# Routed layers: the shared pieces leave the expert loop, and the first 1024 tokens, not 512, are normalised behind it

## The chip, the cores and the metric

The kernel runs on one core of one Trainium2 chip. A core has five engines, each with its own in-order instruction stream: TensorE (PE), VectorE (DVE), ScalarE (ACT), GpSimd (POOL) and SyncE (SP, which here only issues DMAs). They meet through semaphores: an instruction that waits stops everything behind it on its own engine. The metric is the device time of the whole program in microseconds (us); lower is better.

## The reference, cut to what matters

2048 tokens of width 256 go through six layers in a row. Each layer normalises `x` and adds its result to `x`:

```
x = x + 0.5 * ffn0(layernorm(x))     # routed0: 16 experts, top 4 of 16 for each token, plus a shared gated MLP
x = x + attn0(layernorm(x))          # attention0: one head over 2048 tokens, causal
x = x + 0.5 * ffn0(layernorm(x))     # routed1: the same weights as routed0
x = x + 0.5 * ffn1(layernorm(x))     # gated0: silu(x Wg * gs) * (x Wu * us), then Wd
x = x + attn1(layernorm(x))          # attention1: 16 heads
x = x + 0.5 * ffn1(layernorm(x))     # gated1
```

In `ffn0` every expert takes at most 128 tokens: their rows are gathered, go through `silu(xg @ w_gate) * (xg @ w_up) @ w_down`, are weighted, and are scatter-added into `y`. The shared part is `silu(x @ sw_gate) * (x @ sw_up) @ sw_down` over all tokens.

## The kernel before

The six stages run one after another on each engine, with no barrier between them: an engine enters the next stage when its own stream does. `x` stays in on-chip memory as 16 tiles of 128 tokens. A **chunk** is 512 tokens (4 tiles), so there are four chunks, 0 to 3. Products in full precision are made of three matmuls over a high and a low part (`products`, L170 to L172).

**Normalising a chunk** (`ChunkNorm`) takes steps on every engine: DVE measures it (`dve_stats`, L245 and L249), POOL raises the variance to the power -0.5 (`pool_inverse`, L262 and L264; in `quick` chunks DVE then refines it, L285 to L291), DVE and ACT write two normalised tiles each (L309, L319), PE turns them (`pe_flip`, L326), ACT writes the high part of the turned chunk (L331) and DVE the low part (L337). A stage's first matmuls on a chunk need that low part.

**A routed stage** runs a fixed list of steps (`Routed.plan_order`), which every engine walks in the same order, doing its own share. The shared MLP is cut into pieces. Piece q (0 to 11, three for each chunk) has a `gate` step and an `up` step on PE, 12 matmuls in all; ACT takes the silu of the gate, DVE multiplies (L928, signal `acted`), then `round` splits the result: ACT L848, DVE L932. `sums` (c, half) are 18 matmuls on PE that finish half a chunk, and DVE adds them to `x` (L937, signal `added`). In the text g, u and s with numbers stand for these steps: g10, u10, s30 (chunk 3, first half).

The experts run in a loop: POOL gathers 128 rows of `xn_rows` (`fetch`, L1095, six buffers), PE turns them (`x`, L731), multiplies (`feed`, L740), turns back (`h`, L749), multiplies down (`down`, L760), and POOL scatter-adds the result with a DMA (`place`, L1102) into one of two arrays `y_rows` in memory, by turns. Place n waits until place n-2 has landed, and fetch n+6 stands just ahead of place n in POOL's stream.

Two constants cut the list of what is left of the shared pieces once the experts can begin: `AMONG` pieces are spread among the experts, `BEHIND` follow them, and two more are laid into the start of the loop. `early` is the number of `up` steps ahead of the experts; only those pieces alternate between two pairs of accumulator banks (`side`). Every later piece uses the first pair, and then u(q) waits until DVE has multiplied piece q-1, and g(q) until ACT has read gate q-1.

**The expert sums reach x** in six transfers and two DVE additions. Chunk 0 of both `y_rows` arrays is fetched into spare rooms by SP (L649) and added by DVE (`grow`, L987). Chunks 1 to 3 are accumulated straight into `x` by POOL's DMAs (`pool_grow`, L1127): first the half from `y_rows[0]`, and the half from `y_rows[1]` only after the first has landed. `GROWN` gives their order. Chunk 0 is normalised for the next stage (`self.first`) among the last pieces: POOL's part stands between the two transfers of chunk 1. Chunks 1 to 3 are normalised inside attention0 (`Attention0.plan_order`) and inside gated0 (the tables `GROWN_NORM` and `GROWN_LATE`, keys are chunk and piece).

In `gated0` each chunk has six pieces of up to 24 matmuls, `up` (c, m), with ACT's silu (L1890) and DVE's product (L1950) behind each; `up` (c, m) waits for the product two pieces back. ACT also rounds the down weights in chunk 0 (L1862), which waits for their load.

Of the kernel before, what the change touches and what calls it, by code (L numbers as in the profile page):

```python
# [100 lines left out]
class Core:  # L101
# [33 lines left out]
    def loads(self, name):  # L135

        return self.flag(name, 16)

    def keep_warm(self, pe, bank, count):

        for _ in range(count):
            pe.matmul(bank.rearrange("p (a b) -> p a b", b=P), self.ident_b[:], self.ident_b[:].unsqueeze(1).broadcast_to([P, BANK // P, P]),
                      start=True, stop=True)

# [243 lines left out]
class Routed:  # L388
# [6 lines left out]

    AMONG, BEHIND = 4, 12

    def __init__(self, core, stack, tag, then, kept, prior=None, start=None, ahead=()):
# [130 lines left out]
    def plan_order(self):  # L529
# [35 lines left out]
        for n in range(NE):  # L565
# [11 lines left out]
            if n < NE - 2:  # L577
# [78 lines left out]
    def pe(self, pe):  # L656
# [23 lines left out]
        for what, *key in self.order:  # L680
# [70 lines left out]
            elif what == "down":  # L751
                n = key[0]
                pe.wait_ge(*self.h_copied[tag, n])
                pe.wait_ge(*self.down_in[n % self.SLOTS][tag, n])
                if n >= 2:
                    pe.wait_ge(*self.weighed[tag, n - 2])
                elif n == 0 and self.early_sums:
                    pe.wait_ge(*self.added[(tag, *self.early_sums[-1])])
                for k in range(IK):
                    done = pe.matmul(self.down_ps[n % 2], self.e_cols[:, n % 2, k * P:(k + 1) * P], self.e_dn[:, n % self.SLOTS, k, :],  # L760
                                     start=k == 0, stop=k == IK - 1)
                done.then_inc(*self.e_downed.one)
            elif what == "flip":
                self.first.pe_flip(pe, 0, key[0], self.first_banks[key[0]])

# [41 lines left out]
    def act(self, act):  # L807
# [28 lines left out]
        for what, *key in self.order:  # L836
# [30 lines left out]
            elif what == "ahead":  # L867
                self.follower.act_ahead(act, *key)
            elif what == "scale":
                self.first.act_rows(act, 0)  # L870
            elif what == "flip":
                self.first.act_flip(act, 0, key[0], self.first_banks[key[0]])

# [20 lines left out]
    def dve(self, dve):  # L894
# [26 lines left out]
        for what, *key in self.order:  # L921
# [66 lines left out]
            elif what == "measure":  # L988
                self.first.dve_stats(dve, 0)
            elif what == "scale":  # L990
                self.first.dve_rows(dve, 0)
            elif what == "flip":
                self.first.dve_rest(dve, 0, key[0], self.first_banks[key[0]])
        self.step.totals[0] += self.steps
# [71 lines left out]
    def pool(self, pool):  # L1066
# [236 lines left out]
class Attention0(Softmax):  # L1303
# [18 lines left out]
    def __init__(self, core, stack, tag, then, kept, prior, add_y=False):  # L1322
# [41 lines left out]
    def plan_order(self):  # L1364
        project = lambda c: [("flip", c, 0), ("flip", c, 1), ("state", c), ("action", c)]

        order = [("stats", 1), ("inverse", 1), ("grow", 2), *project(0)[2:], ("values", 0), ("score", 0, 0, 0), ("peak", 0, 0), ("exp", 0, 0),
                 ("values", 1), ("bias", 0), ("grow", 3)]
        for t in range(NT + 1):

            nc = t // 4 + 1
            if nc < NCH and t % 4 == 0:
                order += [("rows", nc), ("bias", nc)]

# [4 lines left out]
            if nc < NCH and t % 4 == (nc > 1):  # L1379
                order += project(nc)[:2]  # L1380
            if nc < NCH and t % 4 == 1 + (nc > 1):
# [42 lines left out]
    def rests(self, c):  # L1424

        return (self.first if c == 0 else self.norm).lo[self.tag, c, HK - 1]

# [35 lines left out]
    def pool(self, pool):  # L1463
        for step in self.order:
# [6 lines left out]
            elif step[0] == "bias":  # L1471
                c = step[1]
                pool.wait_ge(*self.weights_in["bo"][self.tag])
                x = self.core.x[:, 4 * c:4 * c + 4, :]
                (self.norm if c else self.first).wait_rows(pool, c)
# [117 lines left out]
class Gated:  # L1593
# [23 lines left out]
    def __init__(self, core, stack, tag, prior, add_y=False, result=None, then=None, ahead=()):  # L1617
# [44 lines left out]
        self.norm = ChunkNorm(core, sb, tag, [c for c in range(NCH) if c not in ahead], add_y=add_y, by_act={**late, 1: 2} if add_y else late,  # L1662
                              quick=(1,) if add_y else ())
        self.first = prior.first if add_y else None
# [43 lines left out]

    def sp_ahead(self, sp):
        for m in range(4):  # L1710
            self.sp_up(sp, m)
# [47 lines left out]
    def pe(self, pe):  # L1759
        if self.add_y:  # L1760
            self.core.keep_warm(pe, self.up_ps[:, 3, :], 4)
        for c in range(NCH):
# [13 lines left out]
    def pe_up(self, pe, c, m):  # L1776
        core, tag, where = self.core, self.tag, slice(c * CH, (c + 1) * CH)
        if m == 0 and c == 0 and self.first:
            self.first.wait_turned(pe, c)
        elif m == 0:  # L1780
            self.norm.wait_turned(pe, c)
        if c == 0:
# [29 lines left out]
    def raw(self, m):  # L1812
        if m < 4 and self.add_y:
            return self.prior.norm.xn[:, 4:12, :].rearrange("p a h -> p (a h)").rearrange("p (k w) -> p k w", k=HK)[:, :, self.cols(m)]
        if m < 2:
# [92 lines left out]
    def dve(self, dve):  # L1908
        tag, norm = self.tag, self.norm
        if self.add_y:  # L1910
            norm.dve_stats(dve, 1)
        else:
            follow(dve, self.prior, "pool")
# [53 lines left out]
    def pool(self, pool):  # L1967
        tag = self.tag
        if self.add_y:
            self.prior.pool_grow(pool, 2)  # L1970
            self.prior.pool_grow(pool, 3)
            self.norm.pool_inverse(pool, 1)
        for m in range(4 if self.add_y else 2, I1M):
# [504 lines left out]
def program(nc, src, out):  # L2478
    with ExitStack() as stack:
# [98 lines left out]
```

## Time and profile before

| | us |
|---|---|
| median of 3 runs | 2030.62 |
| lowest, highest | 2028.19, 2030.73 |
| the profiled execution | 2029.83 |
| its span (first to last instruction) | 2028.0 |
| PE busy | 1944.3 (96% of the span) |
| DVE busy | 1431.3 (71%) |
| ACT busy | 1315.5 (65%) |
| POOL busy | 938.6 (46%) |
| mean granted clock of TensorE | 0.992 of full |

The profile gives each engine's busy time, the granted clock of TensorE in tenths of full speed (1.00 is 2.4 GHz, and 1.2 GHz reads as 0.50), and for each instruction what ended the idle time ahead of it. Seen over the span PE is nearly full. The stretches in which it isn't lie at the start and where the two routed stages hand over: routed0 to attention0 at about 120 to 170 us, routed1 to gated0 at about 360 to 430 us. Those are the two places that the change touches.

### The profile page before, as it was taken

Reading aid. Unit: us, or ns where it says so; the run is one execution under the profiler, and the core shown is the slowest. Engines: PE = TensorE matmul, PEld = TensorE weight load, DVE = VectorE, ACT = ScalarE, POOL = GpSimd, SP = SyncE. Lnnn points to the kernel's source line nnn. Section 1 sums busy time; section 2 is a strip of 40 time slices with the busy share of each in tenths; the row PEclk is TensorE's granted clock in tenths of the full one; section 3 lists DMA queues with packets and bytes.
Section 4 is the critical chain, followed back from the end, with each engine's and each line's share of the span. In section 5 each row is a group of like instructions: output and inputs, shape, how many; then the busy total and the mean of one; then the engine's idle time right before and its main releaser. Section 6 shows DMA issues by size and latency. Waiting matters only on the chain.

```text
span 2028.0 us, 40320 instructions
## 1 busy us (share of the span) xinstructions
PE 1944.3 (96%) x13766; PEld 1767.9 (87%) x13766; DVE 1431.3 (71%) x3604; ACT 1315.5 (65%) x3367; POOL 938.6 (46%) x956
## 2 busy tenths in 40 slices
PE   6988989898999999999999999999999999999999
PEld 4768867687899999999999999999999999998888
DVE  8358763655868777786877778687777878777753
ACT  4335623444778777777868777786777778676752
POOL 1642116434445536454553645455364454536242
PEclk9989999999999999999999999999999999999999
DMA  7751058600000000000000000000000000000000
GB/s 266 204 93 22 33 188 213 145 1 9 9 6 9 9 6 4 7 9 6 9 9 7 4 6 9 9 7 9 7 4 7 9 9 7 9 7 1 22 27 32
DMA packets 58601, 73.46 MB, mean 36 GB/s; under 512 B 9760, under 2 KB 45216, under 8 KB 58272
## 3 DMA queue, kind: packets, MB, share of 16 engines
q1 hardware_dynamic: 45920, 55.93, 8.5%
q0 software_dynamic: 12480, 14.95, 4.3%
q8 instruction: 114, 1.87, 0.4%
q14 instruction: 87, 0.71, 0.1%
HBM read 51.06 MB, written 19.80 MB: 35 GB/s over the span
## 4 chain that ended last, share of the span: by engine, by line
PE 60%; DVE 11%; ACT 9%; issue 7%; POOL 7%; DMA 5%; ACTq 0%; SPq 0%; POOLq 0%; DVEq 0%
PE phase_scores L1222 16%; PE phase_ring L1280 9%; PE phase_y L171 5%; PE phase_y L172 5%; PE phase_y L170 5%; PE phase_ring L170 4%; PE phase_ring L172 4%; PE phase_ring L171 4%; ACT phase_p L1254 3%; DMA y_rows<-phase_out,phase_rows 3%; DVE phase_scores L1233 2%; PE phase_up_ps L170 1%; POOL phase_rot L2456 1%; PE phase_up_ps L172 1%; PE phase_up_ps L171 1%
## 5 line engine op out<-in xcount | busy, mean ns | idle before, releaser
L1254 ACT ACTIVATE phase_p<-phase_scores,phase_bias 128x512 f32<-128x512 f32 (+3 forms) x680 | 416.9, 627 | 117.1 <-DVE phase_bias L1242 116.6
L1300 DVE TENSOR_TENSOR phase_pt_lo<-phase_ring,phase_pt_hi 128x512 fp32r<-128x512 f32 (+3 forms) x680 | 390.2, 602 | 89.5 <-ACT phase_pt_hi L1295 85.7
L1295 ACT ACTIVATE phase_pt_hi<-phase_ring 128x512 fp32r<-128x512 f32 (+3 forms) x680 | 342.9, 535 | 105.3 <-PE phase_ring L1280 101.7
L1280 PE MATMUL phase_ring<-sb_ident,phase_p 128*128 128x128 f32 x2312 | 340.3, 274 | 11.8 <-ACT phase_p L1254 6.8
L170 PE MATMUL phase_y<-phase_pt_hi,phase_v_hi 128*128 128x256 f32 (+1 forms) x1152 | 341.3, 296 | 6.5 <-DVE phase_y_lo L2430 6.5
L171 PE MATMUL phase_y<-phase_pt_lo,phase_v_hi 128*128 128x256 f32 (+1 forms) x1152 | 321.3, 279 | 0.0
L172 PE MATMUL phase_y<-phase_pt_hi,phase_v_lo 128*128 128x256 f32 (+1 forms) x1152 | 321.1, 279 | 0.0
L1280 PEld LDWEIGHTS phase_ring<-sb_ident,phase_p 128*128 128x128 f32 x2312 | 271.8, 140 | 51.8 <-ACT phase_p L1254 16.3
L1235 DVE TENSOR_REDUCE phase_peaks<-phase_scores 128x1 f32<-128x512 f32 (+1 forms) x408 | 265.6, 665 | 46.3 <-PE phase_scores L1222 43.9
L2454 POOL TENSOR_TENSOR phase_straight<-phase_rot,late_rope 64x512 f32<-64x512 f32 x128 | 163.5, 1277 | 274.5 <-ACT phase_rot L2323 274.4
L2471 POOL TENSOR_TENSOR sb_x<-sb_x,phase_part 128x512 f32<-128x512 f32 x128 | 165.0, 1289 | 252.9 <-ACT phase_part L2358 246.5
L1222 PE MATMUL phase_scores<-phase_k_hi,phase_q_hi 128*128 128x512 f32 (+3 forms) x640 | 250.7, 392 | 8.3 <-POOL phase_k_lo L2464 5.2
L1222 PE MATMUL phase_scores<-phase_k_hi,phase_q_lo 128*128 128x512 f32 (+3 forms) x640 | 232.3, 363 | 0.0
L1222 PE MATMUL phase_scores<-phase_k_lo,phase_q_hi 128*128 128x512 f32 (+3 forms) x640 | 231.5, 362 | 0.0
L170 PEld LDWEIGHTS phase_y<-phase_pt_hi,phase_v_hi 128*128 128x128 f32 x1152 | 217.9, 189 | 11.7 <-issue 9.7
L171 PEld LDWEIGHTS phase_y<-phase_pt_lo,phase_v_hi 128*128 128x128 f32 x1152 | 218.0, 189 | 1.4
L172 PEld LDWEIGHTS phase_y<-phase_pt_hi,phase_v_lo 128*128 128x128 f32 x1152 | 217.0, 188 | 0.0
L2456 POOL TENSOR_TENSOR phase_rot<-phase_straight,phase_crossed 64x512 f32<-64x512 f32 x128 | 164.2, 1283 | 10.0
L2463 POOL TENSOR_TENSOR phase_q_lo<-phase_rot,phase_q_hi 128x256 fp32r<-128x256 f32 x128 | 94.2, 736 | 147.7 <-ACT phase_k_hi L2333 144.4
L170 PE MATMUL phase_ring<-sb_xt_hi,late_qk_hi 128*128 128x256 f32 x512 | 147.3, 288 | 0.9 <-DVE phase_pt_lo L1300 0.7
L172 PE MATMUL phase_ring<-sb_xt_hi,late_qk_lo 128*128 128x256 f32 x512 | 143.3, 280 | 0.0
L171 PE MATMUL phase_ring<-sb_xt_lo,late_qk_hi 128*128 128x256 f32 x512 | 143.3, 280 | 0.0
(276 smaller groups left out, 4858.2 us busy)
## 6 DMA issues: line engine op xcount, KB each, us to landing
phase_e_up<-expert_up SPq DMA_DIRECT2D x32, 352.0 KB, 4.6
phase_e_dn<-expert_down SPq DMA_DIRECT2D x32, 256.0 KB, 5.1
y_rows<-phase_zero SPq DMA_DIRECT2D x16, 512.0 KB, 7.8
sb_x<-y_rows POOLq DMA_DIRECT2D x12, 512.0 KB, 6.3
xn_rows<-phase_ln_xn SPq DMA_DIRECT2D x8, 512.0 KB, 3.0
late_raw_qk<-qk SPq DMA_DIRECT2D x16, 256.0 KB, 2.7
sb_x<-x SPq DMA_DIRECT2D x4, 512.0 KB, 5.7
phase_e_up<-y_rows SPq DMA_DIRECT2D x4, 512.0 KB, 4.0
```

The lines of the kernel that those rows point to most:

```text
L170: pe.matmul(out, left_hi[c], r_hi, start=first and c == 0, stop=False)
L171: pe.matmul(out, left_hi[c], r_lo, start=False, stop=False)
L172: done = pe.matmul(out, left_lo[c], r_hi, start=False, stop=last and c == n - 1)
L1222: done = pe.matmul(self.scores[:, at:at + n], a, b, start=k == 0, stop=k == len(pairs(n)) - 1)
L1235: dve.tensor_reduce(peak, scores, AX.X, ALU.max).then_inc(*self.peaked.one)
L1254: act.activation(self.p[:, at:at + width], self.scores[:, at:at + width], ACT.Exp, bias=self.bias[:, t % 2:t % 2 + 1], accum_out=self.sums ...
L1280: done = pe.transpose(bank[:, j * P:(j + 1) * P], self.p[:, (4 * place + j) * P:(4 * place + j + 1) * P], self.core.ident[:])
L1295: act.activation(hi, value, ACT.Copy).then_inc(*self.t_hi.one)
L1300: dve.tensor_tensor(lo, value, as_f32(hi), ALU.subtract).then_inc(*self.t_lo.one)
L2454: pool.tensor_tensor(self.straight[:], self.rot[0:64], self.wide(slice(0, 64), g), ALU.mult).then_inc(*self.straightened.one)
L2456: pool.tensor_tensor(self.rot[0:64], self.straight[:], self.crossed[:], ALU.add).then_inc(*self.turned_by_rope.one)
L2471: pool.tensor_tensor(rows, rows, self.part[:], ALU.add).then_inc(*self.added.one)
```

## The change

`AMONG` goes from 4 to 0 and `BEHIND` from 12 to 20. Of the shared steps left when the experts begin, fewer come ahead (`early` falls from 6 to 4), none among them, and more behind. Chunk 1 is now normalised and turned in the routed stage too, by the same object as chunk 0, and the next stage starts with both. On POOL both transfers of chunk 1 now come ahead of the inverse of chunk 0. The four dummy matmuls at the start of attention0 and gated0 (`keep_warm`) are gone. In gated0 chunks 2 and 3 are measured, scaled and turned at earlier pieces, and its first four weight pieces are loaded into tiles 8 to 15 of the old normalised rows, so that SP waits for the last store and turn of those rows first.

```diff
-    AMONG, BEHIND = 4, 12
+    AMONG, BEHIND = 0, 20
...
-        self.first = ChunkNorm(core, sb, then, (0,), after=lambda c: self.grown[tag, 1], like=self.norm, quick=(0,))
-        self.first_banks = [banks[:, b, :] for b in (6, 7)]
+        self.first = ChunkNorm(core, sb, then, (0, 1), after=lambda c: core.loads("y_in1")[then] if c else self.grown[tag, 1], like=self.norm, quick=(0, 1))
+        self.first_banks = [[banks[:, b, :] for b in pair] for pair in ((6, 7), (5, 3))]
...
-        among = {("up", last - 3): [("ahead", 0)], ("round", last - 3): [("ahead", 1)], ("up", last - 2): [("ahead", 2)],
-                 ("round", last - 2): [("ahead", 3)], ("up", last): [("grow", 0)], ("round", last): [("grow", 1), ("measure",)],
-                 ("sums", NCH - 2, 1): [("scale",)], ("sums", NCH - 1, 1): [("flip", 0), ("flip", 1)]}
+        among = {("up", last - 5): [("ahead", 0)], ("round", last - 5): [("ahead", 1)], ("up", last - 4): [("ahead", 2)],
+                 ("round", last - 4): [("ahead", 3)], ("up", last - 3): [("grow", 0)], ("round", last - 3): [("grow", 1), ("measure", 0)],
+                 ("up", last - 2): [("scale", 0), ("measure", 1)], ("up", last - 1): [("scale", 1)],
+                 ("round", last - 1): [("flip", 0, 0), ("flip", 0, 1)], ("round", last): [("flip", 1, 0), ("flip", 1, 1)]}
...
         pool.wait_ge(*self.y_fetched[1][tag])
         self.pool_grow(pool, 0)
-        self.first.pool_inverse(pool, 0)
         pool.wait_ge(*self.placed[1][tag, NE - 1])
         self.pool_grow(pool, 1)
+        self.first.pool_inverse(pool, 0)
+        self.first.pool_inverse(pool, 1)
...
-        self.norm = ChunkNorm(core, sb, tag, range(1, NCH), add_y=add_y, quick=(1,),
+        self.norm = ChunkNorm(core, sb, tag, range(2, NCH), add_y=add_y,
...
-        core.keep_warm(pe, self.scores[:, 3 * BANK:], 4)
...
-    GROWN_NORM = {(0, 1): [("scale", 0, 1)], (0, 2): [("turn", 0, 1)], (1, 0): [("scale", 0, 2)], (1, 1): [("turn", 0, 2)],
-                  (1, 3): [("scale", 0, 3)], (1, 4): [("turn", 0, 3)]}
-    GROWN_LATE = {(0, 4): [("measure", 0, 2), ("invert", 0, 2)], (1, 1): [("measure", 0, 3), ("invert", 0, 3)]}
+    GROWN_NORM = {(0, 5): [("scale", 0, 2)], (1, 0): [("turn", 0, 2)], (1, 2): [("scale", 0, 3)], (1, 3): [("turn", 0, 3)]}
+    GROWN_LATE = {(0, 3): [("measure", 0, 2), ("invert", 0, 2)], (0, 5): [("measure", 0, 3), ("invert", 0, 3)]}
...
+        if self.add_y:
+            sp.wait_ge(*prior.norm.rows_out[prior.tag, NCH - 1])
+            sp.wait_ge(*prior.norm.turned[prior.tag, NCH - 1, HK - 1])
...
-            self.core.keep_warm(pe, self.up_ps[:, 3, :], 4)
...
-            norm.dve_stats(dve, 1)
...
-            gated0 = Gated(core, inner, "gated0", routed1, add_y=True, then="attention1", ahead=(0,))
+            gated0 = Gated(core, inner, "gated0", routed1, add_y=True, then="attention1", ahead=(0, 1))
```

The order of POOL's stream at the end of routed0, before (the first row is the last of the expert places; `DMA sb_x<-y_rows` is a transfer of `pool_grow`):

```order
L1102 DMA y_rows<-phase_out,phase_rows 2176x256 x7
L1127 DMA sb_x<-y_rows 128x4x256
L262 TENSOR_SCALAR phase_ln_var<-phase_ln_mv 128x4
L264 TENSOR_TENSOR phase_ln_rstd<-phase_ln_var,sb_half 128x4
L1127 DMA sb_x<-y_rows 128x4x256
```

The same place in the changed kernel:

```order
L1097 DMA y_rows<-phase_out,phase_rows 2176x256 x7
L1123 DMA sb_x<-y_rows 128x4x256 x2
L256 TENSOR_SCALAR phase_ln_var<-phase_ln_mv 128x4
L258 TENSOR_TENSOR phase_ln_rstd<-phase_ln_var,sb_half 128x4
L256 TENSOR_SCALAR phase_ln_var<-phase_ln_mv 128x4
L258 TENSOR_TENSOR phase_ln_rstd<-phase_ln_var,sb_half 128x4
```

The inverse of chunk 0 moved behind the second transfer, which itself waits for the landing of the first.

ACT's stream at the end of routed0, before (`phase_gate` is a gate's silu, `phase_h_hi` a round, `phase_ln_xn` the scaling of a chunk, `sb_xt_hi` its turned high part):

```order
L842 ACTIVATE phase_gate<-phase_banks 128x512
L848 ACTIVATE phase_h_hi<-phase_mul 128x512
L842 ACTIVATE phase_gate<-phase_banks 128x512
L848 ACTIVATE phase_h_hi<-phase_mul 128x512 x2
L319 ACTIVATE phase_ln_xn<-sb_x,phase_ln_shift,phase_ln_rstd 128x256 x2
L331 ACTIVATE sb_xt_hi<-phase_banks 128x512 x2
```

ACT's stream at the same end in the changed kernel:

```order
L837 ACTIVATE phase_gate<-phase_banks 128x512
L843 ACTIVATE phase_h_hi<-phase_mul 128x512
L313 ACTIVATE phase_ln_xn<-sb_x,phase_ln_shift,phase_ln_rstd 128x256 x2
L837 ACTIVATE phase_gate<-phase_banks 128x512
L843 ACTIVATE phase_h_hi<-phase_mul 128x512
L313 ACTIVATE phase_ln_xn<-sb_x,phase_ln_shift,phase_ln_rstd 128x256 x2
L837 ACTIVATE phase_gate<-phase_banks 128x512
L843 ACTIVATE phase_h_hi<-phase_mul 128x512
L325 ACTIVATE sb_xt_hi<-phase_banks 128x512 x2
L843 ACTIVATE phase_h_hi<-phase_mul 128x512
L325 ACTIVATE sb_xt_hi<-phase_banks 128x512 x2
```

Two gates, g10 and g11, now stand behind a scaling on ACT; before, the only scaling stood behind the last gate.

DVE's stream at the same end in the changed kernel (`phase_mul` is the product of u9, then of u10, `BN_STATS` the measuring of chunk 1):

```order
L923 TENSOR_TENSOR phase_mul<-phase_gate,phase_banks 128x512
L279 TENSOR_TENSOR phase_ln_tmp<-phase_ln_rstd 128x4
L281 SCALAR_TENSOR_TENSOR phase_ln_tmp<-phase_ln_tmp,phase_ln_var 128x4
L283 SCALAR_TENSOR_TENSOR phase_ln_rstd<-phase_ln_tmp,phase_ln_rstd 128x4
L285 SCALAR_TENSOR_TENSOR phase_ln_shift<-phase_ln_mv,phase_ln_rstd 128x4
L303 TENSOR_SCALAR phase_ln_xn<-sb_x,phase_ln_mv,phase_ln_rstd 128x256 x2
L239 BN_STATS phase_ln_stats<-sb_x 128x6 x4
L243 BN_AGGR phase_ln_mv<-phase_ln_stats 128x2 x4
L927 TENSOR_TENSOR phase_h_lo<-phase_mul,phase_h_hi 128x512
L923 TENSOR_TENSOR phase_mul<-phase_gate,phase_banks 128x512
```

The measuring of chunk 1, which before was the first work of the next stage, now stands between the products of u9 and u10.

## Rows read from the trace of the kernel before

**Rows 1.** Timeline of PE around expert 0 of routed0 (start us, us, instruction).
```profile
53.06 0.39 PE L170 MATMUL phase_banks<-sb_xt_hi,kept_up_hi 128*128 128x512 f32 x1
54.45 0.28 PE L170 MATMUL phase_banks<-kept_dn_hi,phase_h_hi 128*128 128x256 f32 x1
...
59.29 0.38 PE L731 MATMUL phase_banks<-sb_ident,phase_x_rows 128*128 128x128 f32 x2
```

**Rows 2.** Timeline of POOL, the first fetch of routed0, and its line's landing time.
```profile
53.23 1.26 POOL L1095 DMA_INDIRECT phase_x_rows<-xn_rows,phase_rows  x1 [32.52 <-DVE phase_rows L1064]
...
DMA to landing us min/median/max: 3.1/3.1/3.1
```

**Rows 3.** The same for routed1, with PE's first turn of an expert.
```profile
295.11 1.14 POOL L1095 DMA_INDIRECT phase_x_rows<-xn_rows,phase_rows  x1 [30.89 <-DVE phase_rows L1064]
...
DMA to landing us min/median/max: 3.8/3.8/3.8
...
301.28 0.38 PE L731 MATMUL phase_banks<-sb_ident,phase_x_rows 128*128 128x128 f32 x2
```

**Rows 4.** Line L1102 (places), landing time: ten from 68 us, then five from 102 us.
```profile
DMA to landing us min/median/max: 4.5/5.7/6.8
...
DMA to landing us min/median/max: 3.7/3.8/3.9
```

**Rows 5.** The chain that ended last, around the last place (start us, us, what).
```profile
115.41 5.92 DMA y_rows<-phase_out,phase_rows
121.35 3.80 DMA phase_e_up<-y_rows
```

**Rows 6.** Timeline of POOL, chunk 1's two transfers, and their line's landing time.
```profile
125.44 1.39 POOL L1127 DMA_DIRECT2D sb_x<-y_rows  x1 [8.20 <-DMA phase_e_up<-y_rows]
...
128.66 1.05 POOL L264 TENSOR_TENSOR phase_ln_rstd<-phase_ln_var,sb_half 128x4 f32<-128x4 f32 x1
131.84 1.38 POOL L1127 DMA_DIRECT2D sb_x<-y_rows  x1 [2.13 <-DMA sb_x<-y_rows]
...
DMA to landing us min/median/max: 5.8/6.0/6.2
```

**Rows 7.** Timeline of DVE and of ACT at the end of routed0.
```profile
118.57 0.69 DVE L928 TENSOR_TENSOR phase_mul<-phase_gate,phase_banks 128x512 f32<-128x512 f32 x1
...
126.43 1.40 DVE L245 BATCH_NORM_STATS2 phase_ln_stats<-sb_x 128x6 f32<-128x256 f32 x4
...
136.41 1.08 ACT L331 ACTIVATE sb_xt_hi<-phase_banks 128x512 fp32r<-128x512 f32 x2 [4.79 <-PE phase_banks L326]
```

**Rows 8.** Timeline of PE, the start of attention0.
```profile
138.38 0.50 PE L170 MATMUL phase_ring<-sb_xt_hi,phase_hi_ws 128*128 128x512 f32 x1 [0.71 <-DVE sb_xt_lo L337]
...
148.65 1.94 PE L326 MATMUL phase_ring<-sb_ident,phase_ln_xn 128*128 128x128 f32 x8 [3.28 <-ACT phase_ln_xn L319]
...
156.26 0.33 PE L1222 MATMUL phase_scores<-phase_a,phase_s 128*128 128x384 f32 x1
```

**Rows 9.** Busy time by window: PE, PEld, DVE, ACT, POOL, granted clock, DMA share, GB/s.
```profile
129.00:135.00 6.00, 6.00 (x30) 6.00 (x31) 2.41 (x8) 1.09 (x2) 2.09 (x2) 0.54 0.53 78
...
420.00:430.00 10.00, 7.58 (x34) 6.00 (x33) 5.11 (x13) 5.93 (x12) 6.53 (x12) 0.90 0.01 2
```

**Rows 10.** Timelines of POOL, PE and ACT, the start of gated0.
```profile
365.12 1.40 POOL L1127 DMA_DIRECT2D sb_x<-y_rows  x1 [3.77 <-DMA phase_e_up<-y_rows]
...
378.00 0.50 PE L170 MATMUL phase_up_ps<-sb_xt_hi,phase_up_hi 128*128 128x512 f32 x1 [0.71 <-DVE sb_xt_lo L337]
...
385.47 0.42 ACT L1862 ACTIVATE phase_dn_hi<-phase_raw_dn 128x256 fp32r<-128x256 f32 x1 [2.80 <-DMA phase_raw_dn<-down]
...
390.59 1.94 PE L326 MATMUL phase_turn_ps<-sb_ident,phase_ln_xn 128*128 128x128 f32 x8 [3.93 <-ACT phase_ln_xn L319]
...
404.30 0.50 PE L170 MATMUL phase_up_ps<-sb_xt_hi,phase_up_hi 128*128 128x512 f32 x1 [0.77 <-DVE phase_act L1950]
...
427.37 1.27 PE L326 MATMUL phase_turn_ps<-sb_ident,phase_ln_xn 128*128 128x128 f32 x8 [2.42 <-ACT phase_ln_xn L319]
```

More of the change, by code:

```diff
@@ L137, in loads @@
         return self.flag(name, 16)
[L139 to L143, printed above, removed]
     def rooms(self, stack, below=None):
@@ L763, in pe @@
             elif what == "flip":
-                self.first.pe_flip(pe, 0, key[0], self.first_banks[key[0]])
+                self.first.pe_flip(pe, *key, self.first_banks[key[0]][key[1]])
     def pe_flip(self, pe, c):
@@ L869, in act @@
             elif what == "scale":
-                self.first.act_rows(act, 0)
+                self.first.act_rows(act, *key)
             elif what == "flip":
-                self.first.act_flip(act, 0, key[0], self.first_banks[key[0]])
+                self.first.act_flip(act, *key, self.first_banks[key[0]][key[1]])
     def act_weights(self, act, n):
@@ L988, in dve @@
             elif what == "measure":
-                self.first.dve_stats(dve, 0)
+                self.first.dve_stats(dve, *key)
             elif what == "scale":
-                self.first.dve_rows(dve, 0)
+                self.first.dve_rows(dve, *key)
             elif what == "flip":
-                self.first.dve_rest(dve, 0, key[0], self.first_banks[key[0]])
+                self.first.dve_rest(dve, *key, self.first_banks[key[0]][key[1]])
         self.step.totals[0] += self.steps
@@ L1365, in plan_order @@
         project = lambda c: [("flip", c, 0), ("flip", c, 1), ("state", c), ("action", c)]
-        order = [("stats", 1), ("inverse", 1), ("grow", 2), *project(0)[2:], ("values", 0), ("score", 0, 0, 0), ("peak", 0, 0), ("exp", 0, 0),
+        order = [("grow", 2), *project(0)[2:], ("values", 0), ("score", 0, 0, 0), ("peak", 0, 0), ("exp", 0, 0),
                  ("values", 1), ("bias", 0), ("grow", 3)]
@@ L1372, in plan_order @@
             if nc < NCH and t % 4 == 0:
-                order += [("rows", nc), ("bias", nc)]
+                order += [("rows", nc)] * (nc > 1) + [("bias", nc)]
             order += {1: [("grow", 4)], 2: [("grow", 5)], 3: [("stats", 2), ("inverse", 2)], 6: [("stats", 3), ("inverse", 3)]}.get(t, [])
@@ L1379, in plan_order @@
             if nc < NCH and t % 4 == (nc > 1):
-                order += project(nc)[:2]
+                order += project(nc)[:2] if nc > 1 else []
             if nc < NCH and t % 4 == 1 + (nc > 1):
@@ L1424, in rests @@
     def rests(self, c):
-        return (self.first if c == 0 else self.norm).lo[self.tag, c, HK - 1]
+        return (self.first if c in self.first.chunks else self.norm).lo[self.tag, c, HK - 1]
     def sp_ahead(self, sp):
@@ L1474, in pool @@
                 x = self.core.x[:, 4 * c:4 * c + 4, :]
-                (self.norm if c else self.first).wait_rows(pool, c)
+                (self.first if c in self.first.chunks else self.norm).wait_rows(pool, c)
                 pool.tensor_tensor(x, x, self.bo[:].unsqueeze(1).broadcast_to([P, 4, H]), ALU.add).then_inc(*self.biased_x.one)
@@ L1661, in __init__ @@
         late = {c: 4 for c in range(NCH)}
-        self.norm = ChunkNorm(core, sb, tag, [c for c in range(NCH) if c not in ahead], add_y=add_y, by_act={**late, 1: 2} if add_y else late,
-                              quick=(1,) if add_y else ())
+        self.norm = ChunkNorm(core, sb, tag, [c for c in range(NCH) if c not in ahead], add_y=add_y, by_act=late)
         self.first = prior.first if add_y else None
@@ L1709, in sp_ahead @@
     def sp_ahead(self, sp):
+        prior = self.prior
+        if self.add_y:
+            sp.wait_ge(*prior.norm.rows_out[prior.tag, NCH - 1])
+            sp.wait_ge(*prior.norm.turned[prior.tag, NCH - 1, HK - 1])
         for m in range(4):
@@ L1759, in pe @@
     def pe(self, pe):
-        if self.add_y:
-            self.core.keep_warm(pe, self.up_ps[:, 3, :], 4)
         for c in range(NCH):
@@ L1777, in pe_up @@
         core, tag, where = self.core, self.tag, slice(c * CH, (c + 1) * CH)
[L1778 to L1781, printed above, removed]
+        if m == 0:
+            (self.first if self.first and c in self.first.chunks else self.norm).wait_turned(pe, c)
+        if m == 0 and c == 0 and self.add_y:
+            pe.wait_ge(*self.prior.added[self.prior.tag, NCH - 1, 0])
         if c == 0:
@@ L1813, in raw @@
         if m < 4 and self.add_y:
-            return self.prior.norm.xn[:, 4:12, :].rearrange("p a h -> p (a h)").rearrange("p (k w) -> p k w", k=HK)[:, :, self.cols(m)]
+            return self.prior.norm.xn[:, 8:16, :].rearrange("p a h -> p (a h)").rearrange("p (k w) -> p k w", k=HK)[:, :, self.cols(m)]
         if m < 2:
@@ L1909, in dve @@
         tag, norm = self.tag, self.norm
-        if self.add_y:
-            norm.dve_stats(dve, 1)
-        else:
+        if not self.add_y:
             follow(dve, self.prior, "pool")
```

1 line of the change is left out of this document (removed).

## The prediction, made before the changed kernel was run

> **What bounds the kernel now.** I read the page's busy shares first: PE is busy for 96% of the span, so a change can only matter where PE waits or runs slowly. The second view is PE's timeline, searched for idle time. After the experts it waits at the start of attention0 (3.28 us for the scaling of chunk 1 [rows 8]) and of gated0 (3.93 us for chunk 1, 2.42 us for chunk 3 [rows 10]). The third view, busy time by window, shows that waiting costs twice: in 129 to 135 us, right after a wait at the end of routed0, the granted clock is 0.54, which is mostly the lower level of 1.2 GHz, with PE busy all the time [rows 9]. The last view is the chain that ended last. Between the last place and the next stage it holds no PE work at all but DMAs: the last place takes 5.92 us, the fetch of chunk 0's sums 3.80 us [rows 5], and then POOL's two transfers into chunk 1 follow one another, 125.44 and 131.84 us [rows 6]. What the reader is to see: a handover is a chain of landings, and shared pieces are what PE does meanwhile.
>
> **The start of the experts.** Fewer pieces ahead let PE reach its first turn of expert rows earlier, but that turn also needs the first fetch. In routed0 it is issued at 53.23 and lands 3.1 us later, at 56.3 [rows 2]; the turn now starts at 59.29 [rows 1]. PE, with u4 ending at 54.45 [rows 1], waits 1.9 us for it, and the gain is 3.0, not the 4.8 that the pieces are worth. From the turn to the first place two pieces (2 x 1.4 us by 53.06 to 54.45 [rows 1]) give way to one `sums` (2.05) and a handoff of ACT and DVE that nothing covers any more (0.8 estimated), so that way keeps its length. In routed1 the fetch is issued at 295.11 and lands after 3.8, at 298.9, against a turn at 301.28: 2.4 earlier [rows 3].
>
> **Among the experts.** Place n+2 waits for the landing of place n. The places land after 5.7 us in the median, later after 3.8 [rows 4], and with some 0.7 us to the next issue that sets the pace of the loop, not PE. Taking four pieces (two of 1.4, two of 2.05 us) out of the loop therefore buys nothing: PE only waits for fetches instead, and has that work left behind the loop. The bounds: 0, or, if landings became short, a loop bound by POOL's issues, which is a rival below. I take 0. So the end of the places, and with it the issue of the first transfer of chunk 1, which I call F, moves by the start alone: from 125.44 to 122.5 [rows 6], in routed1 from 365.12 to 362.7 [rows 10].
>
> **Behind the experts.** Here the change puts waits in front of PE. POOL issues the second transfer 6.4 us after the first (125.44 to 131.84) and it lands 6.2 us after that, F+12.6; its inverse of chunk 0 now stands behind both issues [rows 6]. ACT waits for that inverse before the silu of g10, about F+10, and g11 on PE waits for that silu. DVE stands in `measure` of chunk 1 until F+12.6; behind it wait the product of u10, so u11 on PE. Measuring takes 1.8 us (1.40 and the aggregation, 0.4) [rows 7]: M = F+14.4. From M everything is one string over ACT and DVE:
> - DVE's rest and product, 1.2; beside them POOL's inverse (1.05 [rows 6] and 0.2) and DVE's refinement, 0.8: M+2.2;
> - ACT's scaling of chunk 1, 1.1, the silu of g11, 0.6, round 10, 0.5, the two high parts of chunk 0, 1.1 (1.08 for two [rows 7]): M+5.6;
> - DVE's last low part, then the product of u11 (0.69 [rows 7]): M+7.0;
> - ACT's round 11 and the two high parts of chunk 1: M+8.7; DVE's last low part: M+9.4; its add of s20, which stands behind these: M+10.0;
> - s30, which needs the bank that this add frees, and s31, 2.05 each: M+14.1.
> So attention0 starts at F+28.5 = 151.0, gated0 at 391.2. Before it is 138.38 [rows 8] and 378.00 [rows 10].
>
> **What the next stage gives back.** Attention0 now has both chunks. Up to the end of chunk 1's projections PE needs four projections and two values (6 x 1.4), scores and one turn (0.5) and one wait (0.8): 9.7 us, so 160.7. Before it was there at 156.26 [rows 8]. Routed0 to attention0: +4.4 us. The clock: PE waits about 6 us ahead of g11. A wait of that kind is followed by the low clock [rows 9]; u11, the turns and s20 at 1.2 GHz add 4.5 us, of which all but 0.7 lies beside ACT and DVE's string. I add 0.7, with 0 and 4.5 as ends.
>
> In gated0 the wait for chunk 1 is gone, but ACT still has to wait for the down weights (385.47, which is 7.5 us after the start [rows 10]), 0.35 us of which reaches PE. The growth of chunk 2 is issued behind POOL's first rest, about 9.8 us in, and lands after 6.6, and DVE now measures chunk 2 at piece (0,3) and stands there from 13.3 to 16.4 us. PE's `up` (1,0) waits 3.2 us for the product behind it. The inverse of chunk 2 then ends at 21.7 and ACT's scaling at 23.8, and the turn, moved ahead to (1,0), waits 2.1 us. `up` (1,1) starts after 19.3 us of work and 5.7 of waits, 25.0, at 416.2. Before it started at 404.30, with the turn (1.1 us) still to do, so 405.4 [rows 10]: +10.8. Given back is the wait of 2.42 us at 427.37 [rows 10] and the low clock after it (0.90 over 10 us, which is 2 us at half speed, 1.0 us lost [rows 9]). Routed1 to gated0: +7.4 us.
>
> **Costed at nothing.** The eight dummy matmuls lie in time in which PE waits for a low part anyway [rows 8, 10]. SP's new wait is for a store long landed when its next job, the expert weights, comes. The gates that are now on one side wait for a silu of 0.6 us behind a piece of 1.4.
>
> **A rule of the skill.** The second transfer's landing rests on 5.8 and 6.2 us for 512 KB [rows 6]. The Trainium skill, page "DMA: Bandwidth & Descriptors", section "Anatomy of one DMA — SWDGE (gpsimd) path", gives about 2.0 us plus the bytes over 436 GB/s, an estimate of 3.2 us here. By it both waits of a handover would be 5.6 us shorter together, and the sum +1.3 us instead of +12.5, about 2031. It is measured on a plain transfer; these add to what is there, and the rows decide.
>
> **The sum.** 4.4 + 0.7 + 7.4 = +12.5 us on the profiled execution's 2029.83: 2042.3. The profiled execution is 0.8 us under the median of the runs, within their spread of 2.5, so I leave it at that.
>
> **Rivals.**
> - *The leg of landings is hidden, faster.* PE has 17 steps behind the experts, 11 gates and ups (15.4 us), six sums (12.3) and two chunks' turns (2.0), 29.7 us. Begun no later than the last place is issued, 115.41-3.0 = 112.4 [rows 5], they end at 142.1, 8.9 ahead of my 151.0. If chunk 1 were ready in time the two handovers would cost 4.4-8.9 and 7.4-8.9, together -6.0: 2023.8. The point is a leg shorter by 6.3 us in each routed stage. For it speaks how much PE work now lies there; against it that ACT and DVE are in order and stand in the waits [rows 6, 7].
> - *The loop speeds up, no change.* If every place landed in 3.8 us, POOL's issues (3.17 us an expert for ten, 2.25 for six) would set the pace and F would come 4.5 us earlier in each stage: +3.5, 2033.3. The late places show 3.8 [rows 4]; but those ran when the weights and fetches were over, and these still run beside the loop.
> - *The clock, much slower.* If PE stays at 1.2 GHz from g11 to s31, 13 us of work, s31 ends 8.9 us later in each stage: +29.6, 2059.4. It has to stay low for 20 us; in 129 to 135 it lasted some 6 [rows 9].
>
> **How the numbers follow.** My forecast has 0.70, the hidden leg 0.10, the faster loop 0.12, the clock 0.08. A difference of 0.2%, 4 us, is about what a measurement of this kernel tells from none. The loop's case is split: half of it lies under 2034.7. With a small part of my own that makes 0.10 faster, 0.09 within, 0.81 slower. The range leaves out half of the hidden leg and most of the clock case: 2031 to 2053; my forecast's own range is 2036 to 2050, from the clock's ends and a landing more or less in each stage.
>
> **What would show it.** Right: the first place of routed0 near 65.6; the two L1123 transfers at about 122.5 and 129 with no instruction between them; ACT idle from about 122 to 132 ahead of a scaling; PE idle ahead of g11 and u11; attention0's first projection near 151; no turn inside the start of attention0; a wait ahead of `up` (1,0) in gated0. Wrong: F earlier than 120, PE with under 3 us of idle time between 108 and 150, or a start of attention0 before 146.

## The result and the profile after

| | median us | runs | lowest to highest |
|---|---|---|---|
| before, beside it | 2029.91 | 4 | 2028.19 to 2030.73 |
| after | 2052.37 | 4 | 2050.11 to 2052.53 |

The ratio is 1.0113 (95% interval 1.0097 to 1.0129): 22.5 us slower, where 12.5 slower was forecast. The time lies 0.6 us below the upper end of the range (2031 to 2053) and 2.4 us above the 2036 to 2050 that the prediction gave its own forecast. The profiled execution took 2052.53 (span 2050.7, mean granted clock 0.991; before 2029.83, 2028.0, 0.992).

Line numbers of the kernel after are 4 to 8 lower: the gate's silu is L837, the product L923, the find L710, the pick L716, the fetch L1090, the place L1097, the transfer L1123. What stands at the points that the prediction named (us from the span's start; e1 is the first experiment below):

| point | before | forecast | after | e1 |
|---|---|---|---|---|
| routed0: pick on PE | 49.48 | 49.48 | 54.56 | 49.49 |
| first fetch | 53.23 | 53.23 | 57.76 | 52.81 |
| first place | 68.65 | 65.6 | 70.19 | 65.20 |
| F, first transfer of chunk 1 | 125.44 | 122.5 | 124.46 | 119.80 |
| attention0, first projection | 138.38 | 151.0 | 154.33 | 149.76 |
| routed1: pick on PE | 291.47 | | 304.60 | 296.43 |
| F in routed1 | 365.12 | | 376.10 | 367.55 |
| gated0, first projection | 378.00 | | 405.62 | 397.44 |
| attention1, first scores | 500.27 | | 522.27 | 512.39 |

The lengths between them are close to the forecast: from F to the next stage 29.9 and 29.5 us (28.5 forecast; 12.9 before), from attention0's start to the end of chunk 1's projections 9.9 (9.7 forecast; 17.9 before), from gated0's start to the scores of attention1 116.65 (122.27 before; 116.5 is the forecast's 5.8 given back). What the forecast doesn't have is a delay that is already there at the pick, before the first expert. PE's timeline after, from the first find of routed0:

```profile
43.84 1.92 PE L710 MATMUL phase_banks<-phase_hot_low,phase_hot_row 128*128 128x256 bf16 x16
49.01 0.50 PE L164 MATMUL phase_banks<-sb_xt_hi,kept_up_hi 128*128 128x512 f32 x1 [3.25 <-ACT phase_gate L837]
...
51.07 2.97 PE L710 MATMUL phase_banks<-phase_hot_low,phase_hot_tile 128*128 128x256 bf16 x16
54.56 0.70 PE L716 MATMUL phase_banks<-phase_masked,kept_same 128*128 128x256 f32 x2 [0.52 <-DVE phase_masked L958]
```

The same four in the kernel before:

```profile
43.89 1.92 PE L715 MATMUL phase_banks<-phase_hot_low,phase_hot_row 128*128 128x256 bf16 x16
45.56 0.48 PE L170 MATMUL phase_banks<-sb_xt_hi,kept_up_hi 128*128 128x512 f32 x1
...
47.05 1.92 PE L715 MATMUL phase_banks<-phase_hot_low,phase_hot_tile 128*128 128x256 bf16 x16
49.48 0.70 PE L721 MATMUL phase_banks<-phase_masked,kept_same 128*128 128x256 f32 x2 [0.52 <-DVE phase_masked L963]
```

Gate 5 stands between the two finds. Before, it had the second pair of banks, whose last user was piece 3; after, it has the first pair and waits until ACT has read gate 4. And ACT reads gate 4 late. The chain that ended last in the kernel after shows why (start, us, what):

```profile
39.95 1.66 DVE phase_hot_row L943 x8
41.61 2.17 DVE phase_hot_low L946 x16
43.78 2.68 DVE phase_hot_tile L951 x8
46.46 0.69 DVE phase_h_lo L927 x2
47.15 0.43 issue
47.58 0.69 DVE phase_mul L923
...
48.35 0.61 ACT phase_gate L837
...
49.01 0.50 PE phase_banks L164
```

The silu of gate 4 goes into the buffer of gate 2, which DVE's product of piece 2 has to empty, and that product stands behind 6.5 us of marks on DVE. ACT's silu was as late in the kernel before, where nothing on PE waited for it:

```profile
48.41 1.19 ACT L842 ACTIVATE phase_gate<-phase_banks 128x512 f32<-128x512 f32 x2 [6.79 <-DVE phase_mul L928]
```

Behind PE's wait of 3.25 us the clock is lower: here are 50 to 57 us after and before (busy time of PE, PEld, DVE, ACT, POOL; granted clock, DMA share, GB/s).

```profile
50.00:57.00 7.00, 6.48 (x37) 4.61 (x37) 2.62 (x7) 1.63 (x3) 0.00 (x0) 0.77 0.00 0
```

```profile
50.00:57.00 7.00, 6.29 (x46) 5.77 (x46) 4.31 (x9) 1.27 (x3) 3.17 (x3) 1.00 0.15 38
```

From gate 5 to the second find 2.06 us pass instead of 1.49, and from there to the pick 3.49 instead of 2.43. With the wait that makes 3.25 + 0.57 + 1.06 = 4.9 of the 5.1 us. Routed1 has the same wait, again 3.25. Its rank step starts 8.2 us later than before (285.68 against 277.52), its pick 13.1 us later: 5.0 more.

Behind the experts the profile shows what was forecast from [rows 6 to 8]. POOL, ACT and PE after:

```profile
124.46 1.39 POOL L1123 DMA_DIRECT2D sb_x<-y_rows  x1 [6.89 <-DMA phase_e_up<-y_rows]
131.17 1.28 POOL L1123 DMA_DIRECT2D sb_x<-y_rows  x1 [5.31 <-DMA sb_x<-y_rows]
```

```profile
134.70 1.09 ACT L313 ACTIVATE phase_ln_xn<-sb_x,phase_ln_shift,phase_ln_rstd 128x256 f32<-128x256 f32 x2 [9.61 <-DVE phase_ln_shift L285]
...
142.06 1.09 ACT L313 ACTIVATE phase_ln_xn<-sb_x,phase_ln_shift,phase_ln_rstd 128x256 f32<-128x256 f32 x2 [5.28 <-DVE phase_ln_shift L285]
```

```profile
129.43 0.50 PE L164 MATMUL phase_banks<-sb_xt_hi,kept_up_hi 128*128 128x512 f32 x1 [2.69 <-DVE phase_mul L923]
136.32 0.80 PE L164 MATMUL phase_banks<-sb_xt_hi,kept_up_hi 128*128 128x512 f32 x1 [5.24 <-ACT phase_gate L837]
143.30 1.07 PE L320 MATMUL phase_banks<-sb_ident,phase_ln_xn 128*128 128x128 f32 x8 [0.39 <-ACT phase_ln_xn L313]
150.01 0.36 PE L164 MATMUL phase_banks<-kept_dn_hi,phase_h_hi 128*128 128x256 f32 x1 [1.55 <-DVE sb_x L932]
```

The two transfers are 6.7 apart with nothing between, ACT stands 9.61 us ahead of the scaling of chunk 0 with g11 behind it, and PE waits 9.9 us in four places (2.69, 5.24, 0.39 and 1.55). In gated0 `up` (1,0) waits 2.02 at 423.21 and the turn of chunk 2 1.84 at 428.09; the waits of 3.28 and 3.93 for chunk 1 [rows 8, 10] are gone.

### The profile page after: what moved, and what is told of

The parts are those of the page before. It is cut to its first block, busy times and chain, and to the rows that moved or that the text cites. A ratio compares the mean times of both kernels' runs of the same rounds, so it can differ in the third digit from the quotient of the medians.

```text
span 2050.7 us, 40304 instructions
## 1 busy us (share of the span) xinstructions
PE 1946.7 (95%) x13758; PEld 1764.9 (86%) x13758; DVE 1431.3 (70%) x3604; ACT 1315.4 (64%) x3367; POOL 938.6 (46%) x956
## 4 chain that ended last, share of the span: by engine, by line
PE 60%; DVE 12%; ACT 9%; issue 7%; POOL 7%; DMA 5%; ACTq 0%; POOLq 0%; SPq 0%; DVEq 0%
PE phase_scores L1218 16%; PE phase_ring L1276 9%; PE phase_y L166 5%; PE phase_y L165 5%; PE phase_y L164 5%; PE phase_ring L164 4%; PE phase_ring L166 4%; PE phase_ring L165 4%; ACT phase_p L1250 3%; DMA y_rows<-phase_out,phase_rows 3%; DVE phase_scores L1229 2%; DMA sb_x<-y_rows 2%; PE phase_up_ps L164 1%; PE phase_up_ps L166 1%; PE phase_up_ps L165 1%
```

## The experiments

Each ratio is against the kernel before, run beside it on the same chip (medians 2029.91 for after, 2028.64 for e1 to e4, 2028.93 for e5 to e8, 2028.86 for e9 and e10); it can differ by about 0.1% from the quotient of the two medians. The median of before was 1.3 us lower beside e1 and e4 than beside after, and 1.0 lower beside e6, so differences to after taken from the medians, as below, may be about 1 us too large. An interval is 0.2 to 0.45% wide, and a difference of under 4 us between two experiments can't be told from medians. Where it is read from the traces, it rests on one execution of each.

| | what | median us | ratio, 95% interval |
|---|---|---|---|
| after | | 2052.37 | 1.0113, 1.0097 to 1.0129 |
| e1 | after, gate 5 behind the pick | 2042.91 | 1.0062, 1.0045 to 1.0080 |
| e2 | before with the spread alone | 2045.40 | 1.0084, 1.0067 to 1.0101 |
| e3 | after, inverse between the transfers | 2052.97 | 1.0107, 1.0084 to 1.0129 |
| e4 | after, measure of chunk 1 behind the pieces | 2042.51 | 1.0063, 1.0045 to 1.0081 |
| e5 | e2 with e1's edit | 2040.45 | 1.0058, 1.0037 to 1.0078 |
| e6 | e4 with e1's edit | 2033.37 | 1.0022, 1.0010 to 1.0035 |
| e7 | e5, chunk 0's steps early | 2035.42 | 1.0037, 1.0024 to 1.0049 |
| e8 | before, 16 behind, 0 among | 2033.31 | 1.0020, 1.0009 to 1.0031 |
| e9 | before, one pair of banks from piece 4 | 2035.88 | 1.0036, 1.0022 to 1.0050 |
| e10 | e7 with two more pieces in the loop | 2032.65 | 1.0024, 1.0010 to 1.0038 |

**e1, the gate behind the pick.**

```diff
-  ("gate", 4), ("find", 0), ("gate", 5), ("find", 1), ("mask",), ("round", 2), ("pick",)]
+  ("gate", 4), ("find", 0), ("find", 1), ("mask",), ("round", 2), ("pick",), ("gate", 5)]
```

> The kernel after, but the gate of piece 5 is asked for behind the pick instead of between the two finds. Theory A (the 3.25 us wait of TensorE ahead of that gate, the slower clock behind it and the second find behind both are the 10 us that the forecast missed): find 1, the mask and the pick no longer stand behind the gate; in routed0 the mask is taken near 49 (54.56 after), the first fetch goes out near 52.5 (57.76), F at 122.5 to 123 (124.46); the same in routed1; 2052.4 less 2.0 and less 5.2: 2045, within 2043 to 2048. Rival B (the front hardly reaches the end, since the landings of the places set the pace): the fetch comes as early, but F moves by under 1 us in each stage: 2050.5 to 2052.5.

9.5 us came off (2052.37 to 2042.91), which is 0.1 us under A's lower bound. PE in e1:

```profile
46.76 1.92 PE L710 MATMUL phase_banks<-phase_hot_low,phase_hot_tile 128*128 128x256 bf16 x16 [0.76 <-DVE phase_hot_tile L951]
49.49 0.70 PE L716 MATMUL phase_banks<-phase_masked,kept_same 128*128 128x256 f32 x2 [0.81 <-DVE phase_masked L958]
```

The second find now waits only for its own marks, and F moves by 4.66 us, not by 2.0: in these two traces what was lost ahead of the experts (5.1 us at the pick) is carried almost whole to the end of the places. Theory A holds. This kernel comes close to the one that was forecast, the change without the front wait: 2042.9 against 2042.3, or 14.3 us over the before beside it against 12.5. The edit does a little more than take out the wait, since it also moves the gate's own 1.4 us behind the pick; e9 changes the banks alone.

**e9, the same wait put into before.**

```diff
-        self.early = sum(step[0] == "up" for step in order)
+        self.early = 4
```

> The kernel before with one number changed: pieces from the fourth on use one pair of banks, as in the kernel after; every piece stays where it is. Theory A (the front wait alone, without spread or second string, is worth what e1 took off): gate 5 waits 3.25 us for the silu of gate 4 between the two finds, the mask is taken near 54.5 instead of 49.48, the first turn of expert rows comes near 64 instead of 59.29, all of it carried; 4.5 to 5.1 us in each stage, 2038 to 2040. Rival B (the landings of the places hide a later start, so that in before the same wait costs little): under 2034.

```profile
48.79 0.79 PE L170 MATMUL phase_banks<-sb_xt_hi,kept_up_hi 128*128 128x512 f32 x1 [3.25 <-ACT phase_gate L842]
54.21 0.70 PE L721 MATMUL phase_banks<-phase_masked,kept_same 128*128 128x256 f32 x2 [0.52 <-DVE phase_masked L963]
```

7.0 us slower by one number: 2.1 us under A's lower bound and 1.9 over B's bound. The wait and the pick are as A says (3.25 us, the pick 4.7 late), but a part is hidden behind it, as B says: the first place is 4.0 us late (72.64), the last place and attention0's start 3.0 (118.42, 141.34). Routed1 adds 5.1 at its pick (8.1 late), of which 7.0 are left at attention1's first scores. So the wait is a cause by itself, worth 7 us in before; in after, e1's edit is worth 9.5.

**e2 and e5, the spread without the second chunk.** `AMONG, BEHIND = 0, 20` in the kernel before, and in e5 also the diff of e1.

> The kernel before with the spread alone changed: no piece among the experts, 20 behind them; chunk 1 is normalised in the next stage as before. It has the front wait of the kernel after (gate 5 on the side of gate 4) and more TensorE work behind the experts, but not the second string of transfer, measure, scale, turn. Theory A (most of the loss is the string of chunk 1, the spread costs the front wait and what TensorE has to catch up): the work behind the experts ends near 145 (the 154.1 of the kernel after less its 9.9 us of waits there; 138.4 before), the 3.3 us wait for chunk 1 in the next stage goes: +3 in each stage, 2036, within 2032 to 2040. Rival B (the spread is the loss, the string hides beside it): 2047 or more. Rival C (the spread is free, the loss is all of the string): under 2031.

> e2 (the spread alone, chunk 1 normalised in the next stage) with the gate of piece 5 behind the pick as in e1. Theory A (the front wait costs the same 9.5 us beside either way of normalising): 2045.4 less 9.5: 2036, within 2034 to 2038; the first projection of attention0 near 142 (146.63 in e2). The rest over before, 6 to 8 us, is then the price of the spread's TensorE work behind the experts, and e1 less this the price of chunk 1 there. Rival B (the front wait was covered here and only hit the kernel with the second string): 2042 or more.

e2 missed by 9 us, e5 by 4. The start of attention0 came where expected (146.63 in e2, 141.54 in e5), but nothing was given back behind it, for two reasons. POOL's second transfer stood behind chunk 0's inverse, which the order of DVE had put behind round 11 (138.96 and 135.33, 13 us behind the first). And the wait for chunk 1 inside attention0, which I had taken for a wait on that transfer, did not go: 3.29 us in e2, 3.28 in e5. In routed1 even the first transfer was late, which no expectation had: it went out 15.3 us behind the last place (10.3 in before, 9.0 in after), since POOL's share of gated0's weights stands ahead of it and waited for ACT's, which comes with the pieces behind the experts. POOL in e2:

```profile
376.02 1.36 POOL L1836 TENSOR_TENSOR phase_up_lo<-phase_ln_xn,phase_up_hi 128x512 fp32r<-128x512 f32 x1 [10.18 <-ACT phase_up_hi L1821]
```

Without the front wait the spread still costs 11.5 us (e5), and the whole change without the front wait 14.3 (e1). The 2.8 us between the two are within their uncertainty.

**e3, the inverse between the transfers.** POOL's inverse of chunk 0 ahead of the second transfer, as in before.

> The kernel after, with POOL's two steps on chunk 0 between the two transfers of chunk 1, as before, instead of behind both. Theory A (what ends the stage is the string from the second transfer's landing: measure, POOL, scale, turn, then four sums): ACT's scaling of chunk 0 comes about 2.4 to 3.3 us earlier and so do gate 11 and its waits, but TensorE then waits for the turn of chunk 1 as long; no change, 2051 to 2053. Rival B (POOL's order holds ACT, and ACT the gates, and that is the loss): the waits of 2.7 and 5.2 us ahead of up 10 and gate 11 shrink by 3 and come off both stages: 2046.

No change, as A says: the wait ahead of g11 fell from 5.24 to 0.36 us, and the one ahead of the next piece's product came up to 6.74. One wait went and another came, behind the measure of chunk 1 on DVE.

**e4 and e6, the measure behind the pieces.** The diff of e4 (which has e3's too; e6 adds e1's):

```diff
-  ("up", last - 2): [("scale", 0), ("measure", 1)], ("up", last - 1): [("scale", 1)],
-  ("round", last - 1): [("flip", 0, 0), ("flip", 0, 1)], ("round", last): [("flip", 1, 0), ("flip", 1, 1)]}
+  ("up", last - 1): [("scale", 0)], ("round", last - 1): [("flip", 0, 0), ("flip", 0, 1)],
+  ("round", last): [("measure", 1)], ("sums", NCH - 2, 1): [("scale", 1)],
+  ("sums", NCH - 1, 0): [("flip", 1, 0), ("flip", 1, 1)]}
```

> The kernel after, with the inverse of chunk 0 between the transfers and, on DVE and ACT, the measure of chunk 1 behind the last round, its scaling behind the sums of chunk 2, its turn behind the first half of the sums of chunk 3; the next stage waits for that turn. Theory A (TensorE waits 9.9 us in all behind the experts because DVE and ACT stand in the measure and the scaling ahead of products and gates that have their data; the order is at fault, not the transfers): the waits ahead of up 10, gate 11 and the first sum go, the next stage starts near 147 instead of 154.1, 4 to 6 us less in each stage, 2041 to 2045. Rival B (the string of chunk 1 is as long wherever it stands; only the place of the wait changes): the wait appears ahead of the turn of chunk 1 or of the next stage's first product: 2050 to 2053.

> e4 (measure, scaling and turn of chunk 1 behind pieces and sums) with the gate of piece 5 behind the pick as in e1. Theory A (the two losses lie one after the other, so that both come off): 2042.5 less 9.5: 2033, within 2031 to 2036, still above before. Rival B (both act on the same wait, so that the second gives little): 2039 or more. Rival C (the reordered kernel beats before): under 2028.

Both times came out by A: 9.9 us less than after, and 19.0 less together (9.5 + 9.9 = 19.4 were the two apart). That this 9.9 equals the 9.9 us that PE waits in routed0 is chance. PE in e4:

```profile
134.29 1.06 PE L320 MATMUL phase_banks<-sb_ident,phase_ln_xn 128*128 128x128 f32 x8 [1.31 <-ACT phase_ln_xn L313]
141.68 0.36 PE L164 MATMUL phase_banks<-kept_dn_hi,phase_h_hi 128*128 128x256 f32 x1 [0.83 <-DVE sb_x L932]
147.84 1.06 PE L320 MATMUL phase_banks<-sb_ident,phase_ln_xn 128*128 128x128 f32 x8 [3.87 <-ACT phase_ln_xn L313]
```

The 5.24 us ahead of g11 and the wait for the product are gone, and the turn of chunk 0 is at 134.29; 3.87 us of waiting are left ahead of chunk 1's turn in routed0, 0.50 in routed1. So A's "near 147" and its "4 to 6 us in each stage" failed: attention0 starts at 152.29, 2.0 us earlier than in after, and routed1's pick is where it was (304.73, 304.60 in after). Nearly all of the gain lies in routed1, where the next stage starts 22.9 us behind F instead of 29.5. In e6 too the leg behind F in routed0 is as in e1 (29.95 and 29.96 us), and the one in routed1 falls from 29.9 to 24.1.

**e7, e8 and e10, towards a kernel that beats both.** e7 is e5 with the additions of chunk 0 behind up 8 and round 8, its scaling behind up 10 and its turn behind round 10; the steps `ahead`, which prepare the next stage's weights, move up by two pieces too. e8 is the kernel before with `AMONG, BEHIND = 0, 16`, by which two steps leave the loop (13 behind it instead of 11) and none leaves the front. e10 is e7 with `4, 16`, and `ahead` one piece later.

> e5 with the steps on chunk 0 three to four pieces earlier, at the places that they have in the kernel after (adds behind up 8 and round 8, scaling behind up 10, turn behind round 10), and chunk 1 still normalised in the next stage. In e2 POOL could not issue the second transfer before it had done chunk 0's inverse, at 138.96, 13.4 us behind the first; here it goes out near F + 6.5. Theory A (what the spread costs is that chunk 0's steps stood too late, not the TensorE work moved): the wait of 3.3 and 1.3 us for chunk 1 in attention0 goes, and 2.2 us in gated0; 2036 less 8: 2028, within 2025 to 2031. Rival B (the TensorE work behind the experts is the price): no more than 2 us less than e5, 2034 or more.

> The kernel before with no piece among the experts and 16 instead of 12 behind them: the pieces ahead of the experts are as before, and so is the side of gate 5. Theory A (a piece costs the same wherever it stands, the landings of the places set the pace of the loop): the loop is at most 1 to 2 us shorter, the four pieces behind it are 5.7 us of TensorE work against 9.4 us of idle time before, but chunk 0's steps come later with them: 2031 to 2034. Rival B (without pieces the loop is faster by what they cost): 2026 or less. Rival C (TensorE's work behind the experts adds in full): 2038 or more.

> e7 (chunk 0's steps early, gate 5 behind the pick, chunk 1 normalised in the next stage) with two more pieces inside the loop and 15 instead of 17 behind it. Theory A (the loop goes by the landings, two pieces of 1.4 us cost nothing inside it and 2.8 us behind): e7's 2035.4 less 2 x 2.8: 2030, as before within the measurement. Rival B (TensorE is full inside the loop too, 50.5 of 54 us, so that the pieces only change place): 2034 to 2036. Rival C (the shorter front and the early steps beat before): 2026 or less.

e7 came out between the two: 5 us less than e5, where B allowed 2, but not A's 2031 or less. A part of its gain is the first transfer of routed1, which with `ahead` moved up goes out 9.8 us behind the last place instead of e5's 15.3. The second transfer does go out early (125.77, and it lands within 6.4 us), and still attention0 waits for chunk 1 as in e2. ACT in e7:

```profile
149.87 1.09 ACT L319 ACTIVATE phase_ln_xn<-sb_x,phase_ln_shift,phase_ln_rstd 128x256 f32<-128x256 f32 x2 [1.42 <-DVE phase_ln_shift L291]
```

PE behind it:

```profile
151.10 1.94 PE L326 MATMUL phase_ring<-sb_ident,phase_ln_xn 128*128 128x128 f32 x8 [3.29 <-ACT phase_ln_xn L319]
```

DVE measures chunk 1 at 140.88, long after the landing, and refines it at 149.09, behind its work on chunk 0. So that wait comes from the order of steps inside attention0, not from a transfer. In these runs it is gone only where the chunk is normalised ahead of the stage; another order inside attention0 wasn't tried. e8's time came out by A, though A had counted four pieces where two steps moved, and e10 between A and B; in e10 the two steps in the loop cost nothing over both stages (first to last place 43.55 and 45.88 us, in e7 45.21 and 44.79). e6, e8 and e10 are the best three, all with an interval above 1: no kernel tried beats the one before.

The second chunk with the old spread wasn't run; its price stands here only as the difference of e1 and e5.

## Why the prediction was right in sign and 10 us short

**Costed at nothing: wrong, and nearly the whole miss.** The failed step is "The gates that are now on one side wait for a silu of 0.6 us behind a piece of 1.4." I took the wait to be for the silu that runs right behind its piece. Gate 5 waits for the silu of gate 4, which had its input from 43.7 on and started at 48.35, since ACT waited for DVE, and DVE stood in the marks. It costs 3.25 us and then 1.6 more, nearly all by the lower clock, in each routed stage; e1 takes off 9.5 us, e9 shows 7.0 by that wait alone. The idle time of 6.79 us that ACT has ahead of that silu could be read in the profile before, too. The other two terms at nothing show no cost: attention0 and gated0 begin at a granted clock of 1.00 without the dummy matmuls, and PE waits for no load at either start.

**That the time lies in the range is luck.** No part of the range stood for this wait. Its upper end was kept for the clock case, which didn't come.

**The start of the experts: right but for this wait.** With the front nearly as assumed (e1) the first place is at 65.20, 65.6 forecast.

**Among the experts: right in size, in part by luck, and not in reason.** From the first place to F it takes 54.3 us in routed0 and 56.1 in routed1, before 56.8 and 54.5: 2.5 less and 1.6 more, which nearly cancel and of which the forecast had neither. The loop itself, first to last place, takes 45.8 and 47.1 us after, 46.8 and 44.2 before. And the landings are not what sets its pace. POOL after:

```profile
70.19 1.63 POOL L1097 DMA_INDIRECT y_rows<-phase_out,phase_rows  x1 [0.30 <-issue]
72.13 1.00 POOL L1090 DMA_INDIRECT phase_x_rows<-xn_rows,phase_rows  x1 [0.30 <-issue]
73.43 1.60 POOL L1097 DMA_INDIRECT y_rows<-phase_out,phase_rows  x1 [0.30 <-issue]
75.33 0.99 POOL L1090 DMA_INDIRECT phase_x_rows<-xn_rows,phase_rows  x1 [0.30 <-issue]
76.63 1.57 POOL L1097 DMA_INDIRECT y_rows<-phase_out,phase_rows  x1 [0.30 <-issue]
```

A place, a fetch and two pauses are 3.2 us, and POOL has no other idle time in these first places: its own issues set the pace. Over the whole loop of routed0 it waits 5.9 us more, 3.5 of them until DVE has an expert's output and 2.0 for landings, all of these near the end; in routed1 7.2, 2.9 and 4.1. So a start lost ahead of the loop is for the most part lost at its end too: 4.7 of 5.1 us in e1, 3.3 of 4.7 in e9 (pick and F of routed0).

**Behind the experts, and what the next stages give back: right.** The two legs were forecast at 28.5 us and measured 29.9 and 29.5, the returns at 9.7 and 116.5 and measured 9.9 and 116.65. The experiments add what a sum could not tell: that a part of the string's length is its order. Where POOL's inverse stands between the transfers makes no difference (e3), but with the measure behind the pieces 9.9 us come off (e4), nearly all in routed1. Why routed0 gains so much less stays open.

**The lower clock behind the experts** was put at 0.7 us. From 137 to 150 us the granted clock is 0.81, and the leg is 1.4 and 1.0 us longer than forecast; how much of that is the clock was not separated.

**The rivals.** The loop did not speed up, the leg behind it was not hidden, and the clock was not what made the 10 us: the wait came first, and where e1 removes it the clock from 50 to 57 us is 1.00 again.

## What to carry to other kernels

When a change moves a buffer from one of two alternating places to one, the new wait is not for the last user's work but for the moment at which the engine that frees it gets to it: look up in the profile when that is, and what stands ahead of it on that engine and on the one that it waits for. A step that waits for a transfer is better placed behind the steps that don't (e4); what two chunks in one string cost depends on their order. And where POOL issues all transfers of a loop, count its issues before blaming landings or TensorE.

## What the runs showed of the hardware that was not expected

- One wait of 3.25 us on PE, behind 10 us of nearly full work at a granted clock of 1.00, was followed by 0.50 from 50 to 53 us and 0.77 over 50 to 57 (1.00 in before): 1.6 us more, half the wait again. The same wait in routed1 of after and in both routed stages of e9 was also followed by a lower clock (0.50 over 299 to 302 us in after). Waits of 0.76 and 0.81 us at the same place (e1) left it at 1.00.
- In routed0 the last place took 5.92 us to land in the kernel before [rows 5] and 3.76 in the one after, the accumulating transfers of 512 KB behind it 6.1 and 6.5 us (5.8 to 6.2 before [rows 6]).
